# Expert stages of a macaron block: down projection in three rounded passes, combine weights on VectorE

## The reference

```
logits = xn @ gate_w.T                      # 8 experts
combine = the two largest softmax values, divided by their sum, others 0
g = xn @ w_gate[e];  u = xn @ w_up[e]       # 176 hidden per expert
out = sum_e combine[e] * ((silu(g) * u) @ w_down[e])
out += sigmoid(xn @ shared_gate_w.T) * ((silu(xn @ sw_gate) * (xn @ sw_up)) @ sw_down)
x = x + 0.5 * out
```

## Time and profile before

| | us |
|---|---|
| median of 3 runs | 2076.58 (2074.81 to 2076.8) |
| the profiled execution | 2074.9 |
| its span, first to last instruction | 2073.1 |
| PE busy | 1854.9 (89% of the span) |
| DVE busy | 1523.3 (73%) |
| ACT busy | 1297.5 (63%) |
| POOL busy | 333.6 (16%) |

### The profile page before, as it was taken

One profiled execution on the slowest core, in us unless ns is written; L12 is line 12 of the kernel. 1 busy time (PEld: TensorE's weight loads), 2 busy tenths in 40 slices (PEclk: granted clock), 3 DMA queues, 4 the chain that ended last, 5 costly groups with the idle time before them and its releaser, 6 DMA issues. The chain is left out here.

```text
span 2073.1 us, 28446 instructions
## 1 busy us (share of the span) xinstructions
PE 1854.9 (89%) x10619; PEld 700.9 (34%) x10619; DVE 1523.3 (73%) x1691; ACT 1297.5 (63%) x2497; POOL 333.6 (16%) x394
## 2 busy tenths in 40 slices
PE   4699996579999999999999999999999998679999
PEld 3466664412222222222222222222222222456665
DVE  6333336489999999999999999999999961633333
ACT  2222224507888888888888888888888885222222
POOL 2355550300000000000000000000000000035554
PEclk9899997858999999999999999999999998689999
DMA  4543310300100000000000010000000001057663
GB/s 107 107 128 110 113 49 16 124 29 2 34 18 18 32 21 18 26 27 18 21 32 18 18 33 19 18 29 23 18 22 30 18 3 49 0 120 131 116 118 62
DMA packets 65155, 98.23 MB, mean 47 GB/s; under 512 B 12013, under 2 KB 31026, under 8 KB 65018
## 3 DMA queue, kind: packets, MB, share of 16 engines
q1 hardware_dynamic: 60858, 94.32, 18.3%
q10 hardware_dynamic: 4160, 2.10, 0.4%
HBM read 84.94 MB, written 11.04 MB: 46 GB/s over the span
## 5 line engine op out<-in xcount | busy, mean ns | idle before, releaser
L1260 DVE TENSOR_REDUCE at_mx<-ps 128x1 f32<-128x1024 f32 x1024 | 1206.5, 1220 | 76.3 <-PE ps L1178 37.8
L1135 ACT ACTIVATE at_prob<-ps 128x512 f32<-128x512 f32 x2048 | 1057.1, 602 | 201.8 <-PE ps L1196 189.5
L1178 PE MATMUL ps<-k_head,q_head 48*128 48x512 bf16 x2048 | 711.8, 395 | 30.4 <-PEq L773 23.5
L1196 PE MATMUL ps<-q_head,k_head 51*128 51x512 bf16 x1924 | 581.7, 383 | 75.8 <-ACT at_prob L1135 34.0
L1206 PE MATMUL ps<-at_prob,vals 128*32 128x512 f32 x4096 | 546.4, 605 | 0.1
L682 DVE TENSOR_TENSOR e_hidden<-e_part,ps 128x512 f32<-128x512 f32 (+1 forms) x208 | 143.0, 688 | 323.6 <-POOL e_part L659 318.6
L1196 PEld LDWEIGHTS ps<-q_head,k_head 51*128 51x128 bf16 x1924 | 143.1, 94 | 687.4 <-ACT at_prob L1135 579.1
L633 ACT ACTIVATE e_silu<-ps 128x512 f32<-128x512 f32 (+1 forms) x208 | 124.4, 598 | 323.5 <-PE ps L591 323.4
L659 POOL TENSOR_TENSOR e_part<-e_silu,e_cw 128x512 f32<-128x512 f32 (+1 forms) x208 | 264.3, 1271 | 380.4 <-ACT e_silu L633 200.5
L1178 PEld LDWEIGHTS ps<-k_head,q_head 48*128 48x128 bf16 x2048 | 150.8, 94 | 205.9 <-DVE at_mx L1260 179.8
L599 PE MATMUL ps<-e_hidden,wdown 128*128 128x512 f32 (+1 forms) x416 | 214.9, 599 | 2.0 <-DVE e_hidden L682 2.0
(11 more groups left out here) (171 smaller groups left out, 926.0 us busy)
## 6 DMA issues: line engine op xcount, KB each, us to landing
e_cw<-comb_rows SPq DMA_DIRECT2D x80, 256.0 KB, 4.4
e_cw<-comb_rows SPq DMA_DIRECT2D x32, 224.0 KB, 6.1
e_cw<-comb_rows SPq DMA_DIRECT2D x32, 192.0 KB, 5.1
q_head<-q_rows SPq DMA_DIRECT2D x64, 96.0 KB
k_head<-k_rows SPq DMA_DIRECT2D x64, 96.0 KB
e_cw<-comb_rows SPq DMA_DIRECT2D x32, 160.0 KB, 4.6
e_cw<-comb_rows SPq DMA_DIRECT2D x48, 96.0 KB, 3.8
e_cw<-comb_rows SPq DMA_DIRECT2D x32, 128.0 KB, 6.3
```

The costliest lines, as they stand in the source:

```text
L1135: act.activation(prob[:, g % PROBS, c, :], ps[:, S + bank(i, g, c, last), :], ACT.Exp).then_inc(exped, 1)
L1178: one = pe.matmul(ps[:, at, :], q[i][HALF:HALF + KR, (j // CHUNKS) * P:(j // CHUNKS + 1) * P], k[i][HALF:HALF + KR, c * BLK:(c + 1) * BLK] ...
L1196: pe.matmul(ps[:, S + bank(i, g, c, last), :], k[i][0:KS, g * P:(g + 1) * P], q[i][0:KS, c * BLK:(c + 1) * BLK], start=True, stop=True).th ...
L1260: dve.tensor_reduce(mx[i][:, j // 2, j % 2:j % 2 + 1], ps[:, at:at + 2, :].rearrange("p a t -> p (a t)"), AX.X, ALU.max).then_inc(max_redu ...
```

## The change

The down projection is done like the up projection. `wdown` becomes a "hi" and a "lo" tensor in fp32r; its raw copy is a third weight that ACT rounds and POOL subtracts in the first norm phase. `hidden` becomes a hi and a lo tensor with three buffers each, and `down` makes three fp32r passes.

The work per chunk on the other engines becomes a longer chain. DVE multiplies silu by the up bank (`prod`), which frees the banks (`product`, what PE's `up` and ACT's SiLU wait for), and then multiplies `prod` by `cw` into `full`. ACT copies `full` to `hidden` hi, which rounds it, after the SiLU of the next chunk in its order. POOL subtracts `full` - hi into `hidden` lo and signals `hidden_ready`, what `down` waits for. The `full` of chunk n waits until POOL has finished chunk n-2.

The combine tiles become a ring of CW = 8, reloaded as soon as `full` of the chunk 8 before has read its tile; stores are issued one block later. `combT` now lies in the memory of `v`. The loops' expressions are otherwise the same.

```diff
@@ -105,7 +105,7 @@
         xnT = [sb("xnT" + part, [P, T], F32R) for part in ("_hi", "_lo")]
         wgate = [sb("wgate" + part, [P, CH * P], F32R) for part in ("_hi", "_lo")]
         wup = [sb("wup" + part, [P, CH * P], F32R) for part in ("_hi", "_lo")]
-        wdown = sb("wdown", [P, CH, D])
+        wdown = [sb("wdown" + part, [P, CH, D], F32R) for part in ("_hi", "_lo")]
         ident = sb("ident", [P, P])
         identb = sb("identb", [P, P], BF16)
         block_rows = sb("block_rows", [P, NB, P])
@@ -120,21 +120,21 @@
         norm_w = sb("norm_w", [P, 2])
         rope = sb("rope", [P, 2, BLK])
         logits = sb("logits", [P, NT, E + 1])
-        combT = sb("combT", [E + 1, T])
         v = sb("v", [P, BATCH, HEADS, KT, HD])
+        combT = v[0:E + 1].rearrange("p b h t d -> p (b h t d)")
         q_head = [sb(f"q_head{i}", [P, SEQ], BF16) for i in range(BUFS)]
         k_head = [sb(f"k_head{i}", [P, SEQ], BF16) for i in range(BUFS)]
         vals = [sb(f"vals{i}", [P, KT, 32]) for i in range(BUFS)]
         with ExitStack() as weights_ctx:
             raw_w = [weights_ctx.enter_context(nc.sbuf_tensor("raw_" + w, [P, CH * P], F32))
-                     for w in ("wgate", "wup")] + [flat(wdown)]
+                     for w in ("wgate", "wup", "wdown")]
             w_loaded = [sem("ld_" + w) for w in ("wgate", "wup", "wdown")]
             loaded = sem("ld_loaded")
             load_phase(nc, sem, sb, locals())
             norm_phase(nc, sem, "n1", ps, x, stats, xnT, ident, gateT, logits,
-                       weights=list(zip(raw_w, (wgate, wup), w_loaded, W_DMAS)),
-                       late=((loaded, 16 * 4), (w_loaded[2], 16 * W_DMAS[2])))
+                       weights=list(zip(raw_w, (wgate, wup, wdown), w_loaded, W_DMAS)),
+                       late=((loaded, 16 * 4),))
         comb_stored = sem("r1_comb_stored")
         routing_phase(nc, sem, "r1", ps, logits, rank, ident, combT, comb_rows[0], comb_stored)
         expert_phase(nc, sem, "e1", ps, x, xnT, wgate, wup, wdown, comb_rows[0], comb_stored, ident,
...
@@ -555,20 +557,27 @@
     added = sem(tag + "_added")
     stored = sem(tag + "_stored")
     rows = [P] * (CH - 1) + [TAIL]
-    cw_loaded = [sem(f"{tag}_cw_loaded{c}") for c in range(CH)]
+    CW = 8
+    cw_loaded = [sem(f"{tag}_cw_loaded{c}") for c in range(CW)]
     pieces = []
     for c in range(CH):
         cuts = [0] + [r for r in range(1, rows[c]) if (c * P + r) % I == 0] + [rows[c]]
         pieces.append([(a, b, (c * P + a) // I) for a, b in zip(cuts, cuts[1:])])
+    def cw_count(n):
+        return 16 * sum(len(pieces[m % CH]) for m in range(n % CW, n + 1, CW))
     with ExitStack() as tmp:
         def tb(name, shape, dt=F32):
             return tmp.enter_context(nc.sbuf_tensor(f"{tag}_{name}", shape, dt))
-        cw = tb("cw", [P, CH, BLK])
+        cw = tb("cw", [P, CW, BLK])
         silu = tb("silu", [P, 2, BLK])
-        part = tb("part", [P, 2, BLK])
-        hidden = tb("hidden", [P, 2, BLK])
+        prod = tb("prod", [P, 2, BLK])
+        full = tb("full", [P, 2, BLK])
+        hidden = [tb("hidden" + part, [P, 3, BLK], F32R) for part in ("_hi", "_lo")]
         yT = tb("yT", [P, BLK])
         block = tmp.enter_context(nc.Block())
         GATE, UP, Y, YT = 0, 2, 6, 7
@@ -585,7 +594,7 @@
                 n, i, cols = blk * CH + c, (par + c) % 2, slice(c * P, (c + 1) * P)
                 tokens = bass.ds(blk * BLK, BLK)
                 if not (isinstance(n, int) and n < 2):
-                    pe.wait_ge(hidden_ready, n - 1)
+                    pe.wait_ge(product, n - 1)
                 for bank, w, done in ((GATE, wgate, gated), (UP, wup, upped))[:1 if c == CH - 1 else 2]:
                     for m, (wp, xp) in enumerate(PASSES):
                         last = pe.matmul(ps[:, bank + i, :], w[wp][:, cols], xnT[xp][:, tokens],
@@ -596,8 +605,11 @@
                 pe.wait_ge(hidden_ready, blk * CH + c + 1)
                 if c == 0:
                     pe.wait_ge(summed_kept, blk + PRIME)
-                pe.matmul(ps[:, Y, :], wdown[0:rows[c], c, :], hidden[0:rows[c], (par + c) % 2, :],
-                          start=(c == 0), stop=(c == CH - 1)).then_inc(downed, 1)
+                at = (blk * CH + c) % 3
+                for m, (wp, hp) in enumerate(PASSES):
+                    last = pe.matmul(ps[:, Y, :], wdown[wp][0:rows[c], c, :], hidden[hp][0:rows[c], at, :],
+                                     start=(c == 0 and m == 0), stop=(c == CH - 1 and m == len(PASSES) - 1))
+                last.then_inc(downed, 1)
             def first():
                 for c in range(3):
@@ -628,20 +640,33 @@
                 n, i = blk * CH + c, (par + c) % 2
                 act.wait_ge(gated, n + 1)
-                if not (isinstance(n, int) and n < 2):
-                    act.wait_ge(weighted, n - 1)
+                if n >= 2:
+                    act.wait_ge(product, n - 1)
                 act.activation(silu[0:rows[c], i, :], ps[0:rows[c], GATE + i, :], ACT.Silu).then_inc(silued, 1)
+            def round_hidden(blk, par, c):
+                n = blk * CH + c
+                act.wait_ge(weighted, n + 1)
+                if n >= 3:
+                    act.wait_ge(downed, n - 2)
+                act.activation(hidden[HI][0:rows[c], n % 3, :], full[0:rows[c], (par + c) % 2, :],
+                               ACT.Copy).then_inc(rounded, 1)
             def first():
                 gate(0, 0, 0)
                 gate(0, 0, 1)
+                round_hidden(0, 0, 0)
             def turn(blk, par, last):
-                for c in range(2, CH + 2):
+                for c in range(1, CH + 1):
+                    if c + 1 < CH:
+                        gate(blk, par, c + 1)
+                    elif not last:
+                        gate(blk + 1, 1 - par, c + 1 - CH)
                     if c < CH:
-                        gate(blk, par, c)
+                        round_hidden(blk, par, c)
                     elif not last:
-                        gate(blk + 1, 1 - par, c - CH)
+                        round_hidden(blk + 1, 1 - par, 0)
                 act.wait_ge(downed, (blk + 1) * CH)
                 act.activation(yT[:], ps[:, Y, :], ACT.Copy).then_inc(summed_kept, 1)
@@ -650,36 +675,28 @@
         @block.gpsimd
         def _(pool):
-            def weigh(blk, par, c):
-                n, i = blk * CH + c, (par + c) % 2
-                pool.wait_ge(silued, n + 1)
-                pool.wait_ge(cw_loaded[c], (blk + 1) * (16 * len(pieces[c])))
-                if not (isinstance(n, int) and n < 2):
-                    pool.wait_ge(hidden_ready, n - 1)
-                pool.tensor_tensor(part[0:rows[c], i, :], silu[0:rows[c], i, :], cw[0:rows[c], c, :],
-                                   ALU.mult).then_inc(weighted, 1)
-            for c in range(CH):
-                weigh(0, 0, c)
-            for c in range(CH):
-                weigh(1, 1, c)
-            for it in range(1, NB // 2):
-                for par in range(2):
-                    for c in range(CH):
-                        weigh(it * 2 + par, par, c)
+            for n in range(NB * CH):
+                r = rows[n % CH]
+                pool.wait_ge(rounded, n + 1)
+                pool.tensor_tensor(hidden[LO][0:r, n % 3, :], full[0:r, (n // CH % 2 + n % CH) % 2, :],
+                                   hidden[HI][0:r, n % 3, :].bitcast(F32), ALU.subtract).then_inc(hidden_ready, 1)
         @block.vector
         def _(dve):
             def multiply(blk, par, c):
                 n, i = blk * CH + c, (par + c) % 2
-                dve.wait_ge(weighted, n + 1)
+                dve.wait_ge(silued, n + 1)
                 up = ps[TAIL_UP:TAIL_UP + TAIL, GATE + i, :]
                 if c < CH - 1:
                     dve.wait_ge(upped, blk * (CH - 1) + c + 1)
                     up = ps[:, UP + i, :]
-                if not (isinstance(n, int) and n < 2):
-                    dve.wait_ge(downed, n - 1)
-                dve.tensor_tensor(hidden[0:rows[c], i, :], part[0:rows[c], i, :], up, ALU.mult).then_inc(hidden_ready, 1)
+                dve.tensor_tensor(prod[0:rows[c], i, :], silu[0:rows[c], i, :], up, ALU.mult).then_inc(product, 1)
+                dve.wait_ge(product, n + 1)
+                dve.wait_ge(cw_loaded[n % CW], cw_count(n))
+                if n >= 2:
+                    dve.wait_ge(hidden_ready, n - 1)
+                dve.tensor_tensor(full[0:rows[c], i, :], prod[0:rows[c], i, :], cw[0:rows[c], n % CW, :],
+                                  ALU.mult).then_inc(weighted, 1)
             def first():
                 for c in range(3 + TPB):
@@ -707,28 +724,26 @@
         @block.sync
         def _(sp):
-            def load(blk, c):
+            def load(n):
+                blk, c = divmod(n, CH)
                 for a, b, expert in pieces[c]:
-                    row = comb_rows[expert:expert + 1, bass.ds(blk * BLK, BLK)]
```

(33 more changed lines are left out.)

## The result

The changed kernel takes 2132.8 us (median of 4, 2130.65 to 2134.66) against 2076.02: a ratio of 1.0269, interval 1.0255 to 1.0282. The forecast was 2141, 2105 to 2170. Its profiled execution took 2134.66, with a span of 2132.9.

A forecast was written before the change was run, and what follows sets the result against it. PE was taken to bound the expert stages before, the collision of `full` with POOL after. Stages 26.6 + 32.2, start and end 2, first norm 3.8: +64.6 on 2074.9 is 2139.5; median 1.7 above, 2141, range 2105 to 2170.

The forecast's parts named there:

- `full` against POOL's subtraction: Expert stages: `full`, with two SBUF operands, stands until POOL's subtraction has finished, then runs; two of three caught.
- The rhythm: Expert stages: chunk steps settle at 2.07, 2.18 and 3.16 us in turn, 2.47 on average.
- The blocks: Expert stages: blocks of 32.6 us, 33.3 in the first stage, against 29.27: +26.6 and +32.2 us.
- 0.6 gained: Start of an expert stage: up(2) needs no `cw`, and `down` follows in 2.84 us instead of about 3.4.
- Start and end, +2: Both expert stages: 0.6 us gained at each start, 1.4 lost at each end, more if caught; together +2.
- First norm: First norm: POOL's subtraction for the third weight lies over four DVE normalizations, +3.8 us.
- I count nothing for the clock: PE's new gaps, about 0.5 us a step, do not lower its clock: no time added.
- Nothing between the stages: Attention, the long stretch between the expert stages, is left alone by the change; the sum has no term for it.
- At no cost: Ring of 8, later stores, `combT`, third `hidden` buffer and PE's clock add no time.
- The signs: Profile after: `full` mean 1 us or more, longest near 1.8; PE near 80% busy; one normalization about 3.7 us longer.
- Rival 1: Expert stages: no collision, handoffs bind; step 2.13, block 28.4, about -8 us, 2068; chance 0.07.

The follow-up runs named there:

- experiments 1 and 2: Changed kernel each: 1 is prod_in_psum; 2 does POOL's subtraction on DVE, behind the next chunk's `prod`, POOL idle: 2049.55 us, ratio 0.9871.
- experiment 4: Changed kernel with the third weight's remainder subtracted on DVE at the end of the first norm (wdown_low_on_vector): 2126.73 us, ratio 1.0241.
- prod_in_psum: Changed kernel with `prod` written to two unused PSUM banks, so `full` reads only `cw` from SBUF: 2068.57 us, ratio 0.9961.
- experiment 8: Changed kernel with 13 combine tiles in the ring in place of 8: 2134.04 us, ratio 1.0268.
- psum_lag3: Changed kernel with `prod` in PSUM and `down` one chunk later in PE's order: 2042.81 us, ratio 0.9829.
- experiment 9: Kernel before, with both weight remainders of the first norm subtracted on DVE instead of POOL: 2074.25 us (median of 10), ratio 0.9992.
- psum_lag3_norm: Changed kernel with `prod` in PSUM, `down` one chunk later, and the third weight's remainder subtracted on DVE: 2037.17 us, ratio 0.9809.

## Why the prediction was right, and where its sizes were off

1. **`full` against POOL's subtraction.** Shown by experiments 1 and 2: with one operand in PSUM, or with POOL idle, `full` goes from 1.55 to 0.69 and the slow-down from +2.7% to below zero. The Trainium skill (SBUF — State Buffer, "SBUF: two separate sides") has the same rule, an exclusive lock that goes to whichever starts first. The trace agrees in both directions: `full` took 1.83 where it started at the same time as POOL, and POOL 1.74 where it started 0.11 behind a `full`. The rows of before showed only VectorE standing, but the forecast kept the two apart either way: its cycle of 2.07 + 2.18 + 3.16 = 7.41 leaves 3.52 for one `full` and one subtraction beside its other times, and if `full` alone stood they would take 1.82 + 1.27 = 3.09 at most.
2. **The rhythm.** 2.04, 3.02, 2.20 for a forecast 2.07, 3.16, 2.18. A step was 0.05 too long on average; 0.03 of it are nine passes of 0.227 taken as 0.23. In the first stage the rhythm was another, as said above: beside the bn_stats every `full` was caught.
3. **The blocks, the sum's main term, mis-sized.** "+3.3 x 8 = 26.6" in the second stage: measured +3.05 x 7 and 0.7 for the first block, 22.0. "+4.0 x 8 = 32.2" in the first: +3.38 x 7 and 0.8, 24.5. The four bn_stats, put at 0.7 a block, go with 32.41 - 32.07 = 0.34 between the stages. And the first block is not one of eight: its first chunks wait for the combine tiles, and in the second stage the first `down` follows its tile by 2.75 us (1869.73 to 1872.48) where it took 4.11 (1832.47 to 1836.58) before. "0.6 gained" there was too little, since before the third `up` took 2.08 and not 1.38 (1834.50 to 1836.58), with its last passes 0.42 to 0.43 apart. From the first `down` to the copy the first block then loses 2.1 (28.6 to 30.7), of which the start gives back 1.4.
4. **Start and end, +2.** Measured +0.5 after the last `yT` copy, the rest within the blocks above.
5. **First norm, mis-sized, +3.8.** Measured +6.8. By experiment 4 the standing is 2.4, and the rest goes with the clock. "I count nothing for the clock" holds for the windows in the expert stages (0.99 and 1.00) and failed here, where TensorE has little work anyway.
6. **Nothing between the stages.** The profiled execution lost 6.0 there. From the end of the last `down` to attention's first product the changed kernel shows 113.6 us and ten of the experiments 111 to 113; only the kernel before (108.1) and prod_in_psum (108.7) are shorter. The code there is the same in all, and these two are the ones whose clock was 1.00 in the stretches looked at. See the last section.
7. **At no cost:** the ring (experiment 8) and the clock in the stages held. `combT`, the stores and the third buffer were not tried by themselves; psum_lag3, which has all three, has 2.04 from `down` to `down`, its nine passes and no gap, so they cost nothing that shows within a block.
8. **The signs.** The mean of `full` (1.35), its longest (1.83) and the block ends near 32 came as said. "PE busy near 80% of the stages" did not: it is 89% and 90% (193.12 of 218, 206.74 of 230), because a pass is recorded with 0.39 and the next follows after 0.23, which hides a part of each gap. The normalization was 2.4 us longer, not 3.7.

The 8 us by which the forecast was too long are these: the two stages 12.3 too much (58.8 against 46.5), start and end 1.5 too much, the first norm 3.0 and the stretch between the stages 6.0 too little, which is 4.8 net; and the median lies 1.9 below its profiled execution, where the forecast put it 1.5 above. So the total is nearer than its main term, and that part is luck: two terms that were too small, one of them put at nothing, cover 9 us of the 14 by which the others were too large.

Rival 1 was right about what lies under the collision: 28.11 a block, 2068.57.

## What to carry to other kernels

When an operation of VectorE reads two SBUF operands and GpSimd works at the same time, price it as its own time plus what is left of GpSimd's operation (here less 0.14), and carry that through the queues chunk by chunk; an operand in a spare PSUM bank takes the stall away for the price of one line. Do that before moving work to GpSimd "because it is idle", and see whether VectorE does the same work in half the time. A faster pass on the bound engine pays only if the chain behind it has a step of slack: here all of the 41 us in the blocks came only with the PSUM operand and `down` one chunk later; the PSUM operand alone gave 16 x (29.03 - 28.11) = 15, and the subtraction on VectorE, with blocks of 27.14, gave 30.

## What was not expected of the hardware

- POOL stands for DVE too: 1.74 for a subtraction of 1.28, begun inside a `full`. In both directions the one that stands loses 0.13 to 0.14 less than the time that the other had left: 0.86 of 1.00 for the `full` at 1893.78, 0.45 of 0.58 for the subtraction at 2006.95.
- DVE's form with one SBUF input and two per-partition scalars, the copies of line 363, stands as well: four took 3.52 in place of 1.11 beside POOL's 3.71, and 8.14 beside 7.44.
- A short idle time of TensorE went with a loss larger than itself. In the changed kernel its passes of L377 follow each other 0.23 apart at 43.8, then it stands for 2.42 until 47.21, and from there they are 0.42 to 0.43 apart, with a clock of 0.50 in the windows above, for the next 6 us and more. In wdown_low_on_vector, without that idle time, they stay 0.23 apart. The clock that a row gives is not enough to tell the level here: the window from 29.0 to 42.4 has a clock of 1.00, and yet the passes in it are 0.42 apart, as at the lower level.

```profile
39.36 0.63 PE L377 MATMUL ps<-xnT_lo,gateT_hi 128*128 128x512 f32 x1
39.78 0.63 PE L377 MATMUL ps<-xnT_hi,gateT_lo 128*128 128x512 f32 x1
...
43.81 0.39 PE L377 MATMUL ps<-xnT_lo,gateT_hi 128*128 128x512 f32 x1
44.04 0.40 PE L377 MATMUL ps<-xnT_hi,gateT_lo 128*128 128x512 f32 x1
```

- The query stage, the same code everywhere, had a different clock in different kernels. In two stretches of 25 to 26 us, of which the first begins 26 or 27 us after the last `down`, it was 1.00 and 1.00 in the kernel before and in prod_in_psum, 0.90 and 0.90 in experiment 9, 0.73 and 1.00 in psum_lag3_norm, and 0.90 and 0.70 in the changed kernel. The way from the last `down` to attention took 108.1, 108.7, 111.3, 112.4 and 113.6 us in this order: the two at full clock are the short ones, and no other run had 1.00 in both stretches. So a few us saved ahead of such a stage may or may not arrive: 4.0 became 1.1 in experiment 9. Why is open; no run here separates it.
